# One transformer block on one core: all batches written out in place of loops of two, and the loads of the next stacks behind the store of the third group's row maxima

## The chip, the cores and the metric

The kernel runs on one core of a Trainium2 chip. The metric is the device time of one execution in microseconds (us). The kernel before takes 664.18 us, the median of three runs (663.45 to 664.81).

## What is computed

The reference is one block with adaptive layer norm for x of shape (8, 512, 128): attention with 16 heads of width 8, then a mixture of 8 experts of which each token uses two. Cut to what matters:

```python
mod = (silu(c) @ wmod).reshape(8, 6, 1, -1)            # sa, ca, ga, sb, cb, gb per batch
ga = sign(ga) * max(|ga|, 0.25);  gb likewise
h = layernorm(x) * (1 + ca) + sa
q, k, v = split(h @ w_qkv);  16 heads of width 8
attn = softmax(q @ k^T / sqrt(128));  o = attn @ v
x = x + ga * (o @ w_out)
h = layernorm(x) * (1 + cb) + sb
scores = softmax(h @ w_router);  top 2 of 8, made to sum to 1 -> comb
y = sum over experts e of comb[:, e] * ((silu(h @ w_gate[e]) * (h @ w_up[e])) @ w_down[e])
x = x + gb * y
```

Everything is float32. Attention is taken per batch of 512 tokens; the experts have 176 hidden units each, 8 x 176 = 1408 = 11 tiles of 128.

## The kernel before

**Two stages.** The first goes over the 8 batches and does attention, the projection, the second layer norm and the router. The second goes over the 8 batches again and does the experts. h2 and the router's weights pass between them through scratch memory in HBM (h2T_scr, combT_scr).

**A batch of the first stage** has 16 slots (SLOTS), four for each of four groups of four heads. A slot handles one chunk of 128 queries or keys of a group. In slot t TensorE makes four row scores (L1142: queries on the partitions, for the maxima) for the slot that lies eight further on (AHEAD), four column scores (L1155: keys on the partitions) for slot t, one of the tasks named in TASKS (transposes and projections for the next batch, output of the batch before), and the product of the probabilities with the values (L1169) for slot t - 1. VectorE takes the maximum of each row score (L853). ScalarE makes exp of each column score (L645) and empties the tasks' results. From slot 8 on the row scores are those of the next batch, so the next batch's stacks must be there by then.

**The stacks.** q and k of a batch are cut into three bf16 parts each, which lie under each other on the contraction axis: q_stack and k_stack, 128 partitions x 8 pairs of heads x 512. ScalarE and POOL make the parts in slots 1 to 4 of the batch before. SP stores them to q_scr and k_scr (L308, six stores each) and loads them back in stacked form (L317): first a quarter of each, 256 KB, counted on the semaphore stacked_first, then the rest, 768 KB each, counted on stacked. There are two stacks of each kind, for even and odd batches. TensorE waits for stacked_first ahead of the row scores of slot 0 of a batch (L1137) and for stacked ahead of those of slot 4 (L1139).

**The maxima.** They come in by rows but are needed by columns. POOL cuts a group's maxima into three parts (split_max), TensorE transposes them (L1098), ScalarE copies them out, stores them with its own DMA queue to max_scr (store_max, L657; groups 1, 2, 3 in slots 1, 5, 9, and group 0 of the next batch in slot 13) and a slot later reads them back into three free rows of q_stack (place_max, L664). The column scores of a group wait for that (L1152). The "third group" is group 2: stored in slot 5, read back in slot 6, used from slot 8.

**SP's order in a batch** (body, L391): wait for the last stacks to be loaded, store the parts of the next batch, load the next batch's stacks (load_stacks), in batch 0 load the expert gate weights, then wait for h2T of the batch before (keep_h2T, made in slot 10) and store it, and wait for combT of the batch before and store it.

**The second stage** has 11 tiles (k) per batch. For each TensorE makes gate and up (three float32r products each, product, L1254) and, three tiles behind (LAG), the down product into o_acc. ScalarE applies silu (L809), VectorE multiplies gate by up (L1022) and by the expert weights (L1032, operands in the space of the stacks), ScalarE makes the high part (hid_high, L789) and POOL the low part (hid_low, L601). When the 11 down products of a batch are done ScalarE scales y (L795, at k = 3 of the next block) and TensorE waits for that ahead of its next down product (L1267).

**The loops.** Each engine's program for both stages is written by over_batches (L277): batch 0, then a hardware loop (Fori) whose body holds the batches 2i+1 and 2i+2 and which runs three times, then batch 7. A body is called with its batch number, its parity, and whether it is the first or the last. In the loop the batch number is a register, so semaphore targets and addresses that hold it are computed by the engines' queues while they run; `isinstance(b, int)` tells in the code whether b is a number.

Of the kernel before, what the change touches and what calls it, by code (L numbers as in the profile page):

```python
# [13 lines left out]
def adaln_block(nc, x, w_qkv, w_out, w_router, w_gate, w_up, w_down, c, wmod, out):  # L14
    B, N, C = x.shape
# [103 lines left out]
    with ctx:  # L119
# [3 lines left out]
        def sem(name):  # L123
            return ctx.enter_context(nc.semaphore(name))
# [145 lines left out]
        s = {n: sem(n) for n in names}  # L270
# [5 lines left out]

        def over_batches(eng, body):  # L277

            body(0, 0, True, False)
            with eng.Fori(0, (B - 2) // 2) as i:  # L280
                body(2 * i + 1, 1, False, False)
                body(2 * i + 2, 0, False, False)
            body(B - 1, 1, False, True)

        def group(b, n):

            return NG * b + n
# [3 lines left out]
        def _(sp):  # L291
# [18 lines left out]
            def load_stacks(b, par):  # L310
                if isinstance(b, int) and b == 0:
                    sp.wait_ge(s["more_stored"], 16 * 4)
                sp.wait_ge(s["q_stored"], 16 * STORES * (b + 1))
                sp.wait_ge(s["k_stored"], 16 * STORES * (b + 1))
                for r0, r1, stacked in ((0, G // 2, "stacked_first"), (G // 2, PAIRS, "stacked")):
                    for stack_sb, scr in ((q_stack[par], q_scr), (k_stack[par], k_scr)):
                        sp.dma_start(stack_sb[:, r0:r1, :], scr.rearrange("a m r n -> (a m) r n")[:, r0:r1]).then_inc(s[stacked], 16)  # L317

            def stack(b, par):
                if not (isinstance(b, int) and b == 0):  # L320
                    sp.wait_ge(s["stacked"], 16 * LOADS * b)
                    sp.sem_inc(s["waited"])
                twice = [P, 2, N]
                store_parts(b, q_scr, (q_parts[:, Q_HIGH:Q_MID + 1], q_parts[:, Q_HIGH:Q_MID + 1], q_parts[:, Q_HIGH:Q_LOW + 1:Q_LOW - Q_HIGH]),
                            "q_mid", "q_split", "q_stored")
                store_parts(b, k_scr, (k_parts[:, K_HIGH:K_HIGH + 1].to_broadcast(twice), k_parts[:, K_MID:K_MID + 1].to_broadcast(twice),
                                       k_parts[:, K_LOW:K_HIGH + 1]), "k_mid", "k_split", "k_stored")
                load_stacks(b, par)

            def keep_h2T(b):  # L330
                sp.wait_ge(s["h2T_ready"], b + 1)
                sp.sem_inc(s["waited"])
                sp.dma_start(h2T_scr[bass.ds(b, 1)].rearrange("o c n -> c (o n)"), h2T[:]).then_inc(s["h2T_kept"], 16)

            def keep_combT(b):
                sp.wait_ge(s["combT_ready"], b + 2)
                sp.sem_inc(s["waited"])
                sp.dma_start(combT_scr[bass.ds(b, 1)].rearrange("o e n -> e (o n)"), combT[:]).then_inc(s["combT_kept"], 16)
# [7 lines left out]
            def fetch_h(b):  # L346

                if isinstance(b, int) and b == 0:
                    sp.wait_ge(s["attn_ready"], NO * (B - 1))
                else:  # L350
                    sp.wait_ge(s["h_split"], b)
                sp.wait_ge(s["h2T_kept"], 16 * (b + 1))
                sp.sem_inc(s["waited"])
                sp.dma_start(h_raw, h2T_scr[bass.ds(b, 1)].rearrange("o c n -> c (o n)")).then_inc(s["h_loaded"], 16)

            def spread_weights(b, k):

                if isinstance(b, int) and b == 0:
                    if k in (0, PAIRS):


                        sp.wait_ge(s["exp_done"], UNITS * (B - 1 if k == 0 else B))
                    if k == 0:
                        sp.wait_ge(s["combT_kept"], 16)
                else:
                    if k == 0:
                        sp.wait_ge(s["combT_kept"], 16 * (b + 1))
                    sp.wait_ge(s["weighed_ready"], KT * (b - 1) + k + 1)
                    sp.sem_inc(s["waited"])
                for e, r0, r1 in EXPERT_ROWS[k]:  # L370
                    sp.dma_start(spread[k][r0:r1], combT_scr[bass.ds(b, 1), e, :].to_broadcast([r1 - r0, N])).then_inc(s[f"spread{k}_loaded"], 16)
# [9 lines left out]
            def load_weights(i):  # L381

                if i:
                    sp.wait_ge(s["w_split"], i)
                if i < 2:
                    sp.dma_start(w_raw[:].rearrange("d (e h) -> d e h", e=E), (w_gate, w_up)[i].rearrange("e d h -> d e h")).then_inc(s["w_loaded"], 16)
                else:
                    sp.dma_start(w_raw[:].rearrange("p (k d) -> p k d", k=KT),
                                 w_down.rearrange("e h d -> (e h) d").rearrange("(k p) d -> p k d", p=P)).then_inc(s["w_loaded"], 16)

            def body(b, par, first, last):  # L391
                if not last:
                    stack(b + 1, 1 - par)
                if first:
                    load_weights(0)
                if last:
                    load_weights(1)
                    load_weights(2)
                if not first:
                    keep_h2T(b - 1)  # L400
                if last:
                    fetch_h(0)
                    for k in range(PAIRS):
                        spread_weights(0, k)
                if not first:
                    keep_combT(b - 1)

            over_batches(sp, body)


# [20 lines left out]
            for k in range(PAIRS, KT):  # L431
                spread_weights(0, k)
            over_batches(sp, block_body)
            store_result(B - 1)
            sp.wait_ge(s["result_stored"], 16 * B)
# [3 lines left out]
        def _(pool):  # L439
# [128 lines left out]
            def body(b, par, first, last):  # L568
# [22 lines left out]
                if not first:  # L591
                    score(b - 1)
                    denominator(b - 1)
                    combine(b - 1)

            over_batches(pool, body)


# [742 lines left out]
```

## Time and profile before

| | |
|---|---|
| median of 3 runs | 664.18 us (663.45 to 664.81) |
| profiled execution, its own time | 666.58 us |
| its span, first to last instruction | 664.8 us |
| granted TensorE clock, mean | 0.96 of full speed |
| busy: TensorE, VectorE, ScalarE, POOL | 609.4, 545.0, 443.4, 267.2 us |
| DMA moved | 65.58 MB, mean 99 GB/s |
| instruction packets, queues q8 and q14 | 14 and 30 |
| first stage, up to the last product with the values | about 450 us |

Busy time is the time in which an engine executed an instruction; waits, branches and register instructions don't count. PE is TensorE's matmul side, PEld its weight loads, DVE VectorE, ACT ScalarE, POOL GpSimd, SP the DMA-issuing engine; a name with q behind it (ACTq) is that engine's sequencer, which issues DMAs and does branches and register work. "Idle before" in a row is the engine's idle time just ahead of the instruction, and behind the arrow stands what ended it.

### The profile page before, as it was taken

The page shows a single profiled execution, that of the slowest core. Times are in us where ns is not written, and L with a number is a line of the kernel's source. Part 1 is how long each engine was busy: PE and PEld are TensorE (multiplying, and loading weights), DVE is VectorE, ACT ScalarE, POOL GpSimd, SP SyncE. Part 2 cuts the span into 40 slices and gives each one's busy share as a digit, 9 for nine tenths or more (in the row PEclk, how much of TensorE's full clock was granted, in tenths as well). Part 3 has the DMA queues.
Part 4 walks back from the last instruction along what each step waited for, and adds up shares of the span by engine and source line. Part 5 has one row for each costly group of instructions (what it writes and reads, how often), then busy time and mean ns, then how long its engine had stood idle before and what let it go on. Part 6 is the DMA issues. An engine that isn't in the chain of part 4 may idle for free.

```text
span 664.8 us, 12806 instructions
## 1 busy us (share of the span) xinstructions
PE 609.4 (92%) x3349; PEld 282.7 (43%) x3349; DVE 545.0 (82%) x1033; ACT 443.4 (67%) x843; POOL 267.2 (40%) x384
## 2 busy tenths in 40 slices
PE   4299999999999999999999999898899999999995
PEld 3112223322322322322322322226677777777773
DVE  3698889999998999998999999417788888888884
ACT  1207878878878778878778878875465555555552
POOL 4422012222222222222222212434576786786763
PEclk9757999999999999999999999979899999999997
DMA  7712604404304304304304301154244445344401
GB/s 187 178 56 61 210 4 97 131 19 97 131 20 97 129 18 97 130 19 97 129 18 97 130 19 47 50 156 142 80 129 157 129 136 149 126 142 142 133 26 32
DMA packets 49084, 65.58 MB, mean 99 GB/s; under 512 B 9544, under 2 KB 30544, under 8 KB 49040
## 3 DMA queue, kind: packets, MB, share of 16 engines
q1 hardware_dynamic: 46416, 64.32, 33.3%
q10 hardware_dynamic: 2624, 0.79, 0.5%
q8 instruction: 14, 0.23, 0.1%
q14 instruction: 30, 0.25, 0.1%
HBM read 47.26 MB, written 17.83 MB: 98 GB/s over the span
## 4 chain that ended last, share of the span: by engine, by line
PE 44%; issue 17%; POOL 16%; DVE 12%; ACT 6%; DMA 2%; SPq 1%; ACTq 1%; DVEq 1%; POOLq 0%
PE o_acc L1169 15%; POOL hid_lo L601 14%; PE s_row L1142 12%; PE s_col L1155 7%; DVE negmax L853 7%; ACT probs L645 4%; DVE probs L1032 2%; PE misc L1107 1%; POOL h_lo L607 1%; PE misc L1093 1%; PE misc L1090 1%; SPq L308 1%; PE misc L1123 1%; ACT oT L649 1%; PE misc L1119 1%
## 5 line engine op out<-in xcount | busy, mean ns | idle before, releaser
L853 DVE TENSOR_REDUCE negmax<-s_row 128x1 f32<-128x512 f32 x512 | 321.6, 682 | 37.9 <-PE s_row L1142 37.1
L645 ACT ACTIVATE probs<-s_col 128x512 f32<-128x512 f32 x512 | 273.6, 599 | 75.0 <-PE s_col L1155 72.0
L1142 PE MATMUL s_row<-k_stack,q_stack 64*128 64x512 bf16 x512 | 142.4, 403 | 23.8 <-DMA k_stack<-k_scr 11.0
L601 POOL TENSOR_TENSOR hid_lo<-probs,hid_hi 128x512 fp32r<-128x512 f32 x87 | 128.5, 1493 | 61.3 <-ACT hid_hi L789 61.3
L1169 PE MATMUL o_acc<-probs,v_aug 128*32 128x512 f32 x1024 | 138.1, 612 | 0.0
L1155 PE MATMUL s_col<-q_stack,k_stack 64*128 64x512 bf16 x512 | 132.3, 384 | 6.1 <-ACT probs L645 5.1
L789 ACT ACTIVATE hid_hi<-probs 128x512 fp32r<-128x512 f32 x88 | 55.6, 632 | 86.3 <-DVE probs L1032 86.0
L1142 PEld LDWEIGHTS s_row<-k_stack,q_stack 64*128 64x128 bf16 x512 | 36.0, 93 | 177.7 <-DVE negmax L853 138.5
L1032 DVE TENSOR_TENSOR probs<-probs,q_stack 128x512 f32<-128x512 f32 x56 | 62.3, 1112 | 15.6 <-POOL hid_lo L601 13.5
L509 POOL CAST negmax_parts<-negmax 128x16 bf16<-128x16 f32 x32 | 6.3, 196 | 166.9 <-DVE negmax L853 166.9
L1022 DVE TENSOR_TENSOR probs<-probs,s_col 128x512 f32<-128x512 f32 x88 | 59.6, 677 | 3.0 <-ACT probs L809 1.6
L809 ACT ACTIVATE probs<-s_row 128x512 f32<-128x512 f32 x88 | 51.5, 585 | 6.7 <-PE s_row L1258 5.9
L1155 PEld LDWEIGHTS s_col<-q_stack,k_stack 64*128 64x128 bf16 x512 | 38.1, 95 | 32.3 <-ACT probs L645 21.7
L1032 DVE TENSOR_TENSOR probs<-probs,k_stack 128x512 f32<-128x512 f32 x32 | 43.0, 1344 | 10.4 <-POOL hid_lo L601 9.8
L1256 PE MATMUL o_acc<-hid_hi,wd_hi 128*128 128x512 f32 x88 | 37.7, 428 | 5.6 <-POOL hid_lo L601 4.6
L1169 PEld LDWEIGHTS o_acc<-probs,v_aug 128*32 128x32 f32 x1024 | 20.2, 108 | 41.7 <-ACT probs L645 24.4
L1256 PE MATMUL s_row<-h_hi,wg_hi 128*128 128x512 f32 x88 | 36.2, 412 | 0.0
L1256 PE MATMUL s_col<-h_hi,wu_hi 128*128 128x512 f32 x88 | 35.3, 401 | 0.0
L1257 PE MATMUL o_acc<-hid_lo,wd_hi 128*128 128x512 f32 x88 | 35.3, 401 | 0.0
L1258 PE MATMUL o_acc<-hid_hi,wd_lo 128*128 128x512 f32 x88 | 35.2, 400 | 0.0
L1258 PE MATMUL s_col<-h_hi,wu_lo 128*128 128x512 f32 x88 | 35.1, 399 | 0.0
L1257 PE MATMUL s_col<-h_lo,wu_hi 128*128 128x512 f32 x88 | 35.0, 398 | 0.0
(134 smaller groups left out, 684.6 us busy)
## 6 DMA issues: line engine op xcount, KB each, us to landing
q_scr<-q_parts SPq DMA_DIRECT2D x48, 128.0 KB, 2.4
k_scr<-k_parts SPq DMA_DIRECT2D x48, 128.0 KB, 2.4
q_stack<-q_scr SPq DMA_DIRECT2D x8, 768.0 KB, 6.0
k_stack<-k_scr SPq DMA_DIRECT2D x8, 768.0 KB, 7.4
q_stack<-combT_scr SPq DMA_DIRECT2D x24, 256.0 KB, 3.3
k_stack<-combT_scr SPq DMA_DIRECT2D x16, 224.0 KB, 2.8
q_stack<-combT_scr SPq DMA_DIRECT2D x16, 192.0 KB, 2.8
q_stack<-combT_scr SPq DMA_DIRECT2D x16, 160.0 KB, 2.5
```

The source lines that it names most:

```text
L601: nc.gpsimd.tensor_tensor(hid_lo[k % HIDDEN][:], weighed[(par + k) % 2], hid_hi[k % HIDDEN][:], ALU.subtract).then_inc(s["hid_split"], 1)
L645: nc.scalar.activation(probs[t % 2][:, j, :], s_col[score_bank("col", u)][:], ACT.Exp, scale=INV_SCALE).then_inc(s["exp_done"], 1)
L789: nc.scalar.activation(hid_hi[k % HIDDEN][:], weighed[(par + k) % 2], ACT.Copy).then_inc(s["hid_high"], 1)
L853: nc.vector.tensor_reduce(negmax[n % 2][:, j, qc:qc + 1], s_row[score_bank("row", u)][:], AX.X, ALU.max, negate=True).then_inc(s["row_max" ...
L1022: nc.vector.tensor_tensor(gated[at], gate_act[at], u_ps[at], ALU.mult).then_inc(s["gated_ready"], 1)
L1032: nc.vector.tensor_tensor(weighed[at], gated[at], spread[k], ALU.mult).then_inc(s["weighed_ready"], 1)
L1142: nc.tensor.matmul(s_row[score_bank("row", u)][:], q_stack[par][at:at + KS, head // 2, P * qc:P * (qc + 1)], k_stack[par][at:at + KS, head ...
L1155: nc.tensor.matmul(s_col[score_bank("col", u)][:], k_stack[par][at:at + KS, head // 2, P * kc:P * (kc + 1)], q_stack[par][at:at + KS, head ...
L1169: last = nc.tensor.matmul(o_acc[VW * j:VW * (j + 1), :], values[:, kc, at:at + VW], probs[t % 2][:, j, :], start=first_of, stop=last_of)
L1256: nc.tensor.matmul(out_ps, w_hi[:, k, :], hi[:], start=start, stop=False)
L1257: nc.tensor.matmul(out_ps, w_hi[:, k, :], lo[:], start=False, stop=False)
L1258: return nc.tensor.matmul(out_ps, w_lo[:, k, :], hi[:], start=False, stop=stop)
```

## The change

All eight bodies of both stages are written out for every engine, and the batch number is a plain number in each. On SP the four loads of load_stacks for batch b wait, from batch 1 on, until group 2 of batch b - 1 has its maxima in max_scr.

```diff
         def over_batches(eng, body):
 
-            body(0, 0, True, False)
-            with eng.Fori(0, (B - 2) // 2) as i:
-                body(2 * i + 1, 1, False, False)
-                body(2 * i + 2, 0, False, False)
-            body(B - 1, 1, False, True)
+            for b in range(B):
+                body(b, b % 2, b == 0, b == B - 1)
...
                 sp.wait_ge(s["q_stored"], 16 * STORES * (b + 1))
                 sp.wait_ge(s["k_stored"], 16 * STORES * (b + 1))
+                if not (isinstance(b, int) and b == 0):
+                    sp.wait_ge(s["max_stored"], 16 * (group(b - 1, 2) + 1))
                 for r0, r1, stacked in ((0, G // 2, "stacked_first"), (G // 2, PAIRS, "stacked")):
```

## Rows read from the trace of the kernel before

**Rows 1.** The page, busy time, share of the span and instructions.

```profile
PE 609.4 (92%) x3349; PEld 282.7 (43%) x3349; DVE 545.0 (82%) x1033; ACT 443.4 (67%) x843; POOL 267.2 (40%) x384
```

**Rows 2.** Busy time by stretch, five batches: start:end, length, busy per engine, clock.

```profile
core 0: us, PE busy (x) PEld busy (x) DVE busy (x) ACT busy (x) POOL busy (x), PEclk, DMA share, GB/s
99.90:149.20 49.30, 47.67 (x314) 15.64 (x312) 45.34 (x97) 40.45 (x80) 13.24 (x34) 1.00 0.30 83
149.20:198.65 49.45, 47.63 (x314) 14.96 (x312) 45.32 (x97) 40.45 (x80) 13.17 (x34) 1.00 0.29 84
198.65:249.15 50.50, 47.91 (x314) 15.73 (x312) 45.41 (x96) 40.45 (x80) 13.21 (x34) 1.00 0.28 81
249.15:298.43 49.28, 47.58 (x314) 14.95 (x312) 45.31 (x96) 40.45 (x80) 13.18 (x34) 1.00 0.29 82
298.43:349.02 50.59, 47.94 (x314) 15.79 (x312) 45.42 (x97) 40.45 (x80) 13.23 (x34) 1.00 0.28 81
```

**Rows 3.** Timeline of ScalarE, start of batches 2 and 3: start, length, idle before.

```profile
149.40 1.08 ACT L645 ACTIVATE probs<-s_col 128x512 f32<-128x512 f32 x2 [0.22 <-PE s_col L1155]
...
200.08 1.08 ACT L645 ACTIVATE probs<-s_col 128x512 f32<-128x512 f32 x2 [1.46 <-PE s_col L1155]
```

**Rows 4.** The loop's line L280, 195 to 201 us: count, durations ns, starts.

```profile
L280 ACTq COMPARE_BRANCH  x1: 50/50/50, 197.3 to 197.3; - x1
L280 DVEq FUSED_REGOPS  x1: 85/85/85, 197.6 to 197.6; - x1
...
L280 ACTq FUSED_REGOPS  x1: 68/68/68, 199.9 to 199.9; - x1
```

**Rows 5.** DMA queues of 149.20:198.65, then of 249.15:298.43: packets, MB, share.

```profile
q8 instruction: 3, 0.05, 0.4%
...
q14 instruction: 2, 0.02, 0.1%
```

**Rows 6.** Busy time by stretch, two blocks of the expert stage.

```profile
488.40:513.05 24.65, 24.17 (x104) 18.66 (x104) 21.03 (x24) 13.64 (x25) 18.11 (x13) 1.00 0.44 138
513.05:537.65 24.60, 24.12 (x104) 18.64 (x103) 20.84 (x24) 13.62 (x25) 17.97 (x13) 1.00 0.44 142
```

**Rows 7.** Timeline of TensorE, first down product of blocks 6 and 7.

```profile
611.81 0.40 PE L1258 MATMUL s_col<-h_hi,wu_lo 128*128 128x512 f32 x1
612.38 0.47 PE L1256 MATMUL o_acc<-hid_hi,wd_hi 128*128 128x512 f32 x1 [0.17 <-ACT probs L795]
...
636.44 0.39 PE L1258 MATMUL s_col<-h_hi,wu_lo 128*128 128x512 f32 x1
636.84 0.47 PE L1256 MATMUL o_acc<-hid_hi,wd_hi 128*128 128x512 f32 x1
```

**Rows 8.** Timeline of VectorE, tile 1 of blocks 6 and 7.

```profile
610.30 0.69 DVE L1032 TENSOR_TENSOR probs<-probs,q_stack 128x512 f32<-128x512 f32 x1 [0.20 <-DVE probs L1022]
...
634.76 0.69 DVE L1032 TENSOR_TENSOR probs<-probs,q_stack 128x512 f32<-128x512 f32 x1
```

**Rows 9.** Timeline, batch 3: the third group's store, the first load of SP.

```profile
216.08 0.33 ACTq L657 DMA_DIRECT2D max_scr<-negmax_T  x1
...
216.37 0.34 SPq L317 DMA_DIRECT2D q_stack<-q_scr  x1
```

**Rows 10.** DMAs issued in 215:219, last row in 165:168: KB, us to landing.

```profile
k_stack<-k_scr SPq DMA_DIRECT2D x1, 768.0 KB, 7.3
...
k_stack<-k_scr SPq DMA_DIRECT2D x1, 256.0 KB, 4.2
...
max_scr<-negmax_T ACTq DMA_DIRECT2D x1, 12.0 KB, 1.4
...
k_stack<-k_scr SPq DMA_DIRECT2D x1, 256.0 KB, 5.5
```

**Rows 11.** Timeline of TensorE: first row scores of batch 4.

```profile
224.86 0.44 PE L1142 MATMUL s_row<-k_stack,q_stack 64*128 64x512 bf16 x2
```

**Rows 12.** Busy time by stretch, end of the first stage.

```profile
433.90:440.70 6.80, 6.54 (x24) 0.75 (x23) 1.49 (x15) 3.74 (x9) 3.64 (x6) 0.50 0.89 259
```

## The prediction

> **What bounds the kernel now.** I read the busy table first. TensorE is busy for 92% of the span [rows 1], so the question for every edit is whether it gives TensorE its next matmul sooner. Then I cut the attention stage into batches, each from one batch's first transpose (L1086, slot 0) to the next batch's, and asked for the busy time of each stretch. TensorE is busy for about 47.6 of 49.3 us in each, at a full granted clock, VectorE for 45.3 and ScalarE for 40.5 [rows 2]. So a batch is close to TensorE's own work, but all three engines are so nearly full that a hole of a microsecond on any of them is not made up.
>
> The same rows show something that belongs to the loop. The stretches last 49.30, 49.45, 50.50, 49.28 and 50.59 us [rows 2]. The third begins within a slot of the place where the loop over pairs (1,2), (3,4), (5,6) jumps back for the first time, the fifth where it jumps back for the second time. There are only two taken jumps, since the third test falls through. Their TensorE work is the same (x314).
>
> ScalarE's timeline shows the hole. Where one body simply follows another, the first exp of a batch starts after an idle time of 0.22 us; at the jump it is 1.46 us [rows 3]. The loop's own instructions explain it: ScalarE's branch starts at 197.3 and takes 50 ns, and its next instruction comes at 199.9, about 2.5 us later, while VectorE's branch of the same moment is followed by its next instruction at 197.6 [rows 4]. ScalarE had two exps queued ahead of the branch, which cover about half of that gap; the rest is the 1.2 us.
>
> **The change part by part.**
>
> *The loops written out, attention stage.* Two taken jumps go. Worked out: (50.50 + 50.59) - 2 x 49.30 = 2.49 us [rows 2]. Measured against 49.45 it is 2.19, against 49.28 it is 2.53; I take 2.49. What is late next once the hole is gone is what is late in the other stretches, TensorE itself, and that is already in the 49.30. The Trainium skill ("Runtime: NRT & Kernel Launch", section "Instruction fetch mechanics") says that a taken branch to code outside the two resident pages must wait until the target page has been fetched, and that crossing a page boundary in straight code is mostly hidden; by that rule the trace's 2.5 us on ScalarE are a page fetch, and writing the code out removes it.
>
> *What straight code costs instead.* Bodies 3 to 6 of the attention loop now have to be fetched for the first time, TensorE's too. In the stretch 149.20 to 198.65, the loop's first pass, TensorE's code arrives in three packets of the queue q8; in 249.15 to 298.43, the same body in its second pass, only two packets of the other engines' queue q14 come [rows 5]. The two stretches last 49.45 and 49.28 us, and the first-pass stretch before them 49.30 [rows 2]. So a body that is fetched costs 0.02 to 0.17 us more than one that is resident, and four bodies cost 0.1 to 0.7 us. I take 0.3. The packets are 0.05 MB in a batch, beside some 4 MB of data.
>
> *The loops written out, expert stage.* Cut at the start of the first y scaling (L795) of each block, a block without a jump lasts 24.65 us and one with a taken jump 24.60 [rows 6]. The jumps cost nothing there: ScalarE is busy for only 13.6 us of a block and TensorE for 24.1. But another cost of the loop shows. The last block is already written out. In block 6, inside the loop, TensorE passes from the last up product to the first down product in 612.38 - 611.81 = 0.57 us and waits 0.17 for the y scaling; in the last block it takes 636.84 - 636.44 = 0.40 and no wait is listed [rows 7]. The cause lies on VectorE: in the loop the multiplication by the expert weights (L1032, k = 1) starts after 0.20 us of idle time behind the gating (L1022), in the last block none is listed [rows 8]. In the loop body the wait of L1029 for a register's value is an instruction of its own ahead of it. With constants it can sit in the multiplication. Six blocks (1 to 6) get the form of the last one: 6 x 0.17 = 1.0 us. Bounds: nothing, if another wait of the block takes it over (TensorE's second stall in a block is for POOL's hid_lo), and 6 x 0.26 = 1.6 us, an estimate from half again of the 0.17 for that second stall. I take 1.0.
>
> *Register arithmetic elsewhere.* In attention the loop bodies compute each wait's value in the engines' queues. It runs while their instructions are busy. No row shows a stall from it; I take nothing, with 0 to -0.5 us as bounds.
>
> *The new wait of SP.* It stands in front of the four stack loads, behind the two waits for the stores of q and k. Behind it on SP are the four loads, in the first batch also the weight load (704 KB, needed six batches later), and then the wait for h2T, which comes some 15 us after the loads; nobody else waits in SP's queue. In batch 3 ScalarE issues the third group's store at 216.08 and SP the first load at 216.37 [rows 9]. The store lands 1.4 us after its issue [rows 10], so about 217.5, and counting 0.3 us from landing to the next issue, the loads start at 217.8: 1.4 us later than now. In the first batch (store at 69.0, loads at 70.1 now) the shift is about 0.5 us. Is there room? The half that is needed first lands last with k_stack's 256 KB: issued 0.38 us behind the first load, landing 4.2 us later in this batch and 5.5 in the worst one [rows 10]. That gives 217.8 + 0.4 + 4.2 = 222.4, at worst 223.7. TensorE's first row scores of the next batch start at 224.86 [rows 11]. Room: 2.5 us, at worst 1.2. The second half (768 KB, 7.3 us [rows 10]) would be there at about 226.5 and is read four slots after 224.86, over 12 us later. The cost is zero. It is covered by TensorE's slots 6 and 7, and if that cover went, each microsecond of lateness would cost one in each of seven batches.
>
> What could the wait bring? It takes the loads' packets out of the way of the small store and of the read back into q_stack that follows it. The column scores of slot 8 need that read. No instruction of the trace is listed as waiting for it, and the slots have the same length in the batch where the store took 2.5 us instead of 1.4. So the gain is zero too.
>
> **Sum.** -2.49 + 0.3 - 1.0 + 0 = -3.2 us. Against the profiled execution (666.58 us, of which 664.8 are the span and 1.8 lie around it) that is 663.4; that execution was 2.4 us above the median of the runs, 664.18, to which I apply the same difference: 661.0 us.
>
> **The rivals.**
>
> *The hole is not the jump's.* Only ScalarE shows it; VectorE's restart after 0.4 us [rows 4] speaks for a cheap branch. Then the attention gain is nil and -1.0 + 0.3 leaves 663.5, no measurable change. Against it: both long stretches, and only they, hold a taken jump. The Trainium skill ("Advanced Engine Details and Errata", "Control Flow Timing") puts a compare-and-branch at about 108 ns, by which the four jumps of a program would be worth an estimated 0.4 us; ScalarE's 50 ns agree with the instruction itself, but the 2.5 us behind it do not agree with the idea that this is all.
>
> *Code that comes late.* Straight code must be fetched for every body. If ScalarE, whose queue is short, missed each of its blocks of code as it missed the jump's target, 1.2 us a time, one miss in each of the four newly fetched bodies would cost 4.8 us and turn the sum into +1.6 less the 0.3 already counted: 665.5. It decides from three misses on (3 x 1.2 = 3.6 against the 3.2 gained). Against it: the first-pass stretches fetched their code and lasted 49.30 and 49.45 [rows 2, 5].
>
> *The loads come too late (the other side).* Place: TensorE's row scores at slot 8. It decides once the first k half lands over 2.5 us later than reckoned, for instance if it took as long as the second half's 7.3 us, because the read of q_stack and all four loads now start together. It would land at 225.5, 0.6 us late; with the row scores then behind in each of seven batches, and VectorE with no slack to make it up, 7 x 0.6 = 4.5 us, which gives 665.5. With 2 us late it is 675. Against it: four loads start together now too, at 4.2 to 5.5 us.
>
> *The clock.* Between the stages TensorE's granted clock is 0.50 for 6.8 us with TensorE busy for 6.54 [rows 12]; it fell after a stretch in which TensorE had waited for ScalarE and POOL several times. At full clock that work would take about half, so such a dip is worth up to 3 us. A program that is shorter by 3 us may meet it a little differently, longer or shorter: 658.5 or 663.5.
>
> **How the numbers follow.** What can be told from no change here is 0.2%, 1.3 us. My forecast, 661.0 with its own range 659.6 to 662.6, gets 0.68. The clock 0.14 (0.10 of it still faster, 0.03 the same, 0.01 slower). The hole that isn't the jump's 0.11 (0.09 same, 0.02 slower). Late code 0.04 and late loads 0.03, both slower. So faster 0.78, same 0.12, slower 0.10. The range takes in the bounds of the terms (-2.5 + 0.1 - 1.6 - 0.5 = -4.5 gives 659.7, and -2.2 + 0.7 - 0 = -1.5 gives 662.7) and reaches toward the clock's cases: 658.9 to 663.7.
>
> **What would show it.** Right: ScalarE's first exp of every batch after 0.2 us of idle time; all six stretches between 49.2 and 49.5 us; more packets in the instruction queues, twice as many in q8; blocks 1 to 6 of the expert stage at 24.46 us; first loads about 1.4 us behind the third group's store in each batch, and no instruction waiting for k_stack besides the one at the start. Wrong: a stretch of over 50 us anywhere, or row scores that wait for a DMA in slot 8 (then the loads decide), or blocks that still last 24.6 us (then another wait has taken the 0.17).

## The result: 656.0 us, 8.7 us less than before

Over 20 runs of each, the changed kernel takes 656.02 us (653.28 to 663.60) and the kernel before 664.75 us (661.19 to 668.04). The ratio is 0.9877 with a 95% interval of 0.9857 to 0.9897, that is 6.8 to 9.5 us less. The forecast was 3.2 us less, 661.0 us, with a range down to 658.9. The sign was right, and so were the two gains that the sum named, the jumps and the experts. A third, which the sum put at nothing, was the largest.

The profiled execution took 655.2 us with a span of 653.6. These are its rows, in the views of before. First the busy table, which answers to [rows 1]: TensorE is busy for 8.4 us less with the same number of instructions.

```profile
PE 601.0 (92%) x3349; PEld 277.1 (42%) x3349; DVE 544.0 (83%) x1033; ACT 443.7 (68%) x843; POOL 267.0 (41%) x384
```

The attention batches, cut at the same transposes as in [rows 2] (start:end, length, busy time and count by engine, clock, DMA share, GB/s); the third and the fifth used to hold a taken jump. The last row is the low-clock stretch between the stages, which was 6.8 us long in [rows 12]:

```profile
99.63:148.24 48.61, 47.11 (x314) 14.64 (x313) 45.27 (x97) 40.48 (x80) 13.18 (x34) 1.00 0.30 84
148.24:196.85 48.61, 47.11 (x315) 14.63 (x313) 45.27 (x97) 40.47 (x80) 13.18 (x34) 1.00 0.30 85
196.85:245.45 48.60, 47.10 (x314) 14.63 (x312) 45.25 (x97) 40.47 (x80) 13.18 (x34) 1.00 0.30 84
...
294.06:342.66 48.60, 47.10 (x314) 14.64 (x313) 45.27 (x97) 40.47 (x80) 13.16 (x34) 1.00 0.29 84
421.90:425.30 3.40, 3.21 (x14) 1.02 (x14) 0.00 (x0) 3.12 (x6) 0.04 (x1) 0.51 0.13 46
```

ScalarE's first exp at the place of the former jump (start, length, idle time before it; [rows 3] had 1.46 us), then the instruction queues of the whole program, from the page:

```profile
196.95 1.08 ACT L644 ACTIVATE probs<-s_col 128x512 f32<-128x512 f32 x2 [0.21 <-PE s_col L1154]
```

```profile
q8 instruction: 27, 0.44, 0.3%
q14 instruction: 28, 0.22, 0.1%
```

A block of the expert stage, and TensorE's first down product in the block that was numbered 6 in [rows 7]; and SP's first load behind the third group's store, with its landing, which answer to [rows 9] and [rows 10]:

```profile
576.58:601.04 24.46, 24.13 (x105) 18.65 (x104) 20.78 (x24) 13.63 (x26) 17.99 (x13) 1.00 0.47 142
```

```profile
601.45 0.40 PE L1257 MATMUL s_col<-h_hi,wu_lo 128*128 128x512 f32 x1
601.86 0.47 PE L1255 MATMUL o_acc<-hid_hi,wd_hi 128*128 128x512 f32 x1
```

```profile
212.71 0.33 ACTq L656 DMA_DIRECT2D max_scr<-negmax_T  x1
214.15 0.33 SPq L316 DMA_DIRECT2D q_stack<-q_scr  x1
```

```profile
k_stack<-k_scr SPq DMA_DIRECT2D x1, 256.0 KB, 4.6
```

What the reader is to see: all five stretches are equal, and they are not 49.3 us long, as forecast, but 48.6. TensorE's own busy time in a stretch fell from 47.6 to 47.1 us with the same number of matmuls, so part of what it waited before must have been booked as busy time of its matmuls. The 11.2 us by which the two profiled spans differ are, cut at the first product with the values in each batch: start 0.3, last slots of batch 0 0.2, two jumps 2.5, batches 1 to 6 another 6 x 0.67 = 4.0, batch 7 with the shorter low-clock stretch 2.5, six blocks 1.0, the end at a better clock 0.7. So 4.0 us are not in the forecast's sum. The last batch and the end, some 3 us together, are for the most part the clock (an estimate from the low-clock stretch, 3.4 us instead of 6.8, and from the end). The medians, which average the clock over 20 runs, leave 8.7.

The chain of waits of one batch shows where to look for the missing 4.0 us, but not their size. These are its shares by line, before and then after. "issue" is time in which an engine waited for nothing the profile names: 14.4% of 49.45 us is 7.1 us, of which 1.26 are the hole at the jump; 4.4% of 48.61 is 2.1. The issue time fell by 3.7 us beyond the hole, while the batch got only 0.84 us shorter: most of the rest moved to the shares of TensorE and VectorE.

```profile
by line: PE o_acc L1169 24.2%; PE s_row L1142 15.8%; issue 14.4%; PE s_col L1155 11.7%; DVE negmax L853 9.8%; ACT probs L645 7.6%; PE misc L1107 2.4%; PE misc L1093 2.2%; PE misc L1090 2.1%; PE misc L1123 2.0%; ACT oT L649 1.6%; DVE r_witho
```

```profile
by line: PE o_acc L1168 26.6%; PE s_row L1141 18.9%; DVE negmax L852 13.8%; PE s_col L1154 12.1%; ACT probs L644 5.9%; issue 4.4%; PE misc L1106 2.4%; PE misc L1092 2.2%; PE misc L1089 2.2%; PE misc L1122 2.0%; DVE x_all L879 1.4%; PE misc 
```

### The profile page after: what moved, and what is told of

Its sections match the earlier page's. It is cut to its first block, busy times and chain, and to the rows that moved or that the text cites. A ratio compares the mean times of both kernels' runs of the same rounds, so it can differ in the third digit from the quotient of the medians.

```text
span 653.6 us, 10459 instructions
## 1 busy us (share of the span) xinstructions
PE 601.0 (92%) x3349; PEld 277.1 (42%) x3349; DVE 544.0 (83%) x1033; ACT 443.7 (68%) x843; POOL 267.0 (41%) x384
## 4 chain that ended last, share of the span: by engine, by line
PE 47%; DVE 20%; POOL 15%; ACT 8%; issue 6%; DMA 1%; SPq 1%; POOLq 0%; DVEq 0%; ACTq 0%
PE o_acc L1168 16%; PE s_row L1141 14%; POOL hid_lo L600 11%; DVE negmax L852 8%; DVE probs L1031 7%; PE s_col L1154 7%; ACT probs L644 3%; ACT hid_hi L788 3%; POOL h_lo L606 2%; PE misc L1106 1%; SPq L305 1%; PE misc L1122 1%; PE misc L1092 1%; PE misc L1089 1%; DVE probs L1021 1%
## 5 line engine op out<-in xcount | busy, mean ns | idle before, releaser
L644 ACT ACTIVATE probs<-s_col 128x512 f32<-128x512 f32 x512 | 273.4, 598 | 66.0 <-PE s_col L1154 62.9
L1154 PE MATMUL s_col<-q_stack,k_stack 64*128 64x512 bf16 x512 | 127.8, 381 | 3.3 <-ACT probs L644 2.7
L1154 PEld LDWEIGHTS s_col<-q_stack,k_stack 64*128 64x128 bf16 x512 | 36.2, 95 | 23.0 <-ACT probs L644 15.2
```

The lines of the kernel that those rows point to most:

```text
L644: nc.scalar.activation(probs[t % 2][:, j, :], s_col[score_bank("col", u)][:], ACT.Exp, scale=INV_SCALE).then_inc(s["exp_done"], 1)
L1154: nc.tensor.matmul(s_col[score_bank("col", u)][:], k_stack[par][at:at + KS, head // 2, P * kc:P * (kc + 1)], q_stack[par][at:at + KS, head ...
```

## The experiments

In each, the five attention stretches from the second batch on are added up as the most exact measure: 249.12 us before, 243.03 after. The stretches are from the one profiled execution of each kernel. Times are medians, ratios are to the kernel before on the same chip.

**unroll_only.** All loops written out, without the new wait. Against the kernel after:

```diff
-                if not (isinstance(b, int) and b == 0):
-                    sp.wait_ge(s["max_stored"], 16 * (group(b - 1, 2) + 1))
```

> All bodies written out, without the new wait of SP. Theory R (the loop's registers cost time in every body): all of the gain stays; attention batches last 48.6 us as in the changed kernel, blocks 24.47, time about 656 us, same as the changed kernel within 0.3%. Theory W (the later loads give the unexplained 0.67 us of a batch): batches last 49.2 to 49.3 us, time about 660 us.

Measured: 656.94 us, ratio 0.9872 (0.9838 to 0.9907). Five stretches: 243.00.

```profile
148.93:197.53 48.60, 47.09 (x314) 14.64 (x313) 45.24 (x97) 40.49 (x80) 13.21 (x34) 1.00 0.30 85
```

Within the interval the whole gain is there without the wait.

**wait_only.** The loops of before, with the new wait.

```diff
                 sp.wait_ge(s["k_stored"], 16 * STORES * (b + 1))
+                if not (isinstance(b, int) and b == 0):
+                    sp.wait_ge(s["max_stored"], 16 * (group(b - 1, 2) + 1))
```

> The loops of two stay, only the new wait of SP is added. Theory R: no change, batches of 49.3 us and two of 50.5, time within 0.2% of the kernel before. Theory W: batches of 48.6 us and two of 49.9, time about 660.7 us (664.7 - 4.0).

Measured: 664.01 us, ratio 0.9997 (0.9970 to 1.0024), five stretches 248.71, two of them (50.37, 50.35) with a jump. The wait alone moves nothing. The 4.0 us belong to the writing out.

**hinted_jump.** The loops of before, and the branch's target is fetched ahead.

```diff
-            with eng.Fori(0, (B - 2) // 2) as i:
+            with nc.Fori(0, (B - 2) // 2, engines=bass.OrderedEngineSet([eng.engine]), hint_back_edge=True) as i:
```

> The loops of two stay, with an instruction at the head of each pass that has the code at the jump's target fetched ahead. Theory J (the hole at the jump is ScalarE's missing code): the two stretches of 50.5 us fall to 49.3, ScalarE's idle time there from 1.46 to about 0.22 us, time 2.5 us below before (-0.37%). If the hole is something else in the loop's turn: no change.

Measured: 665.85 us, ratio 1.0015 (0.9986 to 1.0044); stretches 50.49, 49.26, 49.27, 49.26, 49.26. First the loop's own line on ScalarE (against [rows 4]), then ScalarE's first exp behind the jump and a stall in the first stretch.

```profile
L280 ACTq COMPARE_BRANCH  x1: 68/68/68, 198.9 to 198.9; - x1
...
L280 ACTq FUSED_REGOPS  x1: 68/68/68, 199.2 to 199.2; - x1
```

```profile
200.42 1.08 ACT L645 ACTIVATE probs<-s_col 128x512 f32<-128x512 f32 x2 [0.22 <-PE s_col L1155]
```

```profile
126.61 0.09 PEld L1155 LDWEIGHTS s_col<-q_stack,k_stack 64*128 64x128 bf16 x1 [1.09 <-DMA q_stack<-max_scr]
126.61 0.39 PE L1155 MATMUL s_col<-q_stack,k_stack 64*128 64x512 bf16 x1 [0.80 <-DMA q_stack<-max_scr]
```

ScalarE resumes 0.3 us after the branch instead of 2.5, and the stretches with a jump are as long as the others: the hole was the fetch of the jump's target. The gain of 2.5 us does not show in the time, and the profiled execution has two places where it went. One is a stall of 1.2 us in batch 1 (the PE row above), where the store of the third group's maxima took 3.06 us and its read-back 6.56 us to land. The larger one is in the last batch, behind the loop: ScalarE idles for 2.26 us and nothing in the profile says for what; then TensorE runs for 3.0 us at a granted clock of 0.52. That slot lasts 6.64 us instead of 3.17.

```profile
415.50 0.60 ACT L645 ACTIVATE probs<-s_col 128x512 f32<-128x512 f32 x1 [2.26 <-issue]
```

```profile
417.40:420.40 3.00, 3.00 (x13) 1.89 (x12) 0.86 (x2) 1.15 (x3) 0.00 (x0) 0.52 0.00 0
```

Of the thirteen kernels profiled only the two that fetch the branch's target ahead have such a hole there. Two packets of the instruction queue q14 come at 414.0 and 416.2 us, so code that arrives late is likely; that the fetch ahead causes it is not shown. Whether the timed runs lose at the same places can't be seen.

**swapped_waits.** The loops of before. In the exps, the row maxima and the experts' multiplication by the weights, the wait named first is named last.

```diff
-                act.wait_ge(s["col_ready"], UNITS * b + u + 1)
                 if j == 0 and not (isinstance(b, int) and b == 0 and t < 2):
                     act.wait_ge(s["pv_done"], SLOTS * b + t - 1)
+                act.wait_ge(s["col_ready"], UNITS * b + u + 1)
```

> The loops of two stay; where exp (L645), the row maximum (L853) and the weighing (L1032) have several waits, the one that comes true last is now named last, so that it should sit on the instruction itself and the early ones on instructions of the sequencer. Theory R, in the form that only the late wait on an instruction of its own costs time: batches 0.3 to 0.6 us shorter (48.7 to 49.0), blocks 24.47 in place of 24.63, time 3 to 5 us below before, with the two holes of 1.2 us still there. If the register arithmetic itself costs the time, or the addresses: no change in either.

Measured: 665.63 us, ratio 1.0024 (0.9999 to 1.0049). Five stretches 247.77, blocks 24.84.

```profile
247.85:297.01 49.16, 47.43 (x314) 14.86 (x313) 45.23 (x97) 40.64 (x80) 13.16 (x34) 1.00 0.29 83
533.54:558.40 24.86, 24.32 (x105) 18.61 (x104) 20.84 (x24) 13.58 (x26) 18.32 (x13) 1.00 0.49 137
```

The expected 3 to 5 us did not come. Attention gets shorter by 0.1 to 0.5 us a batch, with the registers still there, and the blocks longer by 0.2, which takes back what attention gives. So where a wait stands matters, both ways. It led to the theory for the rest: an instruction holds one wait. Its others stand ahead of it in the queue as instructions of their own. The wait that is met last costs time if it is one of these. In attention's loop, where values come from registers, the wait named first is the one that stands alone, and the kernel names the late one first (col_ready, row_ready). In straight code it is the one named last.

The experts' loop does not follow the first rule. There the swap put the late wait (gated_ready) ahead of the multiplication by the weights instead of on it, and in most tiles that multiplication starts 0.13 us behind the gating (here 536.67 - 536.53 = 0.14), where before it was 0.03 to 0.04. This is why the blocks got longer:

```profile
535.86 0.67 DVE L1022 TENSOR_TENSOR probs<-probs,s_col 128x512 f32<-128x512 f32 x1
536.67 0.69 DVE L1032 TENSOR_TENSOR probs<-probs,q_stack 128x512 f32<-128x512 f32 x1
```

For attention the trace shows it by line for the exps of one batch, before (L644 is the line of pv_done) and then after (L643):

```profile
L644 ACTq ALU_OP  x13: 35/35/35, 156.2 to 196.1; - x13
L644 ACTq EVENT_SEMAPHORE  x2: 17/17/17, 152.7 to 178.5; - x2
```

```profile
L643 ACTq EVENT_SEMAPHORE  x16: 17/17/17, 151.6 to 196.4; - x16
```

After, pv_done stands alone 16 times, long met, and col_ready sits on the exp. Before, pv_done stands alone twice; in the other 14 the instruction that computes pv_done's value (13 ALU_OP, one FUSED_REGOPS) stands ahead of the exp and holds the wait for col_ready. The Trainium skill ("Perfetto Trace Analysis", "Identifying Dependency Chains") says that an instruction that waits for several engines may get EventSemaphore instructions ahead of it; the rows agree (16 of them in a batch after).

**late_wait_alone.** unroll_only with these waits of the exps and row maxima named in the other order, so that in straight code too the late one stands alone. Of the two edits, the one on VectorE:

```diff
-                dve.wait_ge(s["row_ready"], UNITS * b + u + 1)
                 if qc == 0 and j == 0 and not (isinstance(b, int) and b == 0 and n < 2):
                     dve.wait_ge(s["max_split"], 4 * (group(b, n) - 1))
+                dve.wait_ge(s["row_ready"], UNITS * b + u + 1)
```

> Straight code without the new wait, as unroll_only (656.94 us, batches 48.60 us). One thing is changed: in the exps (L645 of before) and the row maxima the two waits are named in the other order, so that the one that is met last (col_ready, row_ready) goes to the sequencer as an instruction of its own, which the profile's list of waits shows for the loop kernels. Theory A (a late wait that stands alone, ahead of its instruction, costs the start of that instruction; the 4.0 us of the result come from where the waits sit): slots 0, 9, 11 and 12 go back from 2.70, 2.96, 3.07, 2.87 towards 2.81, 3.11, 3.15, 2.96 us, batches 48.9 to 49.1, the kernel 2 to 3 us slower than unroll_only: 659 to 660. Theory B (it is the register arithmetic of the loop itself that costs, wherever the waits sit): batches stay at 48.6, the kernel at 657.

Measured: 659.28 us, ratio 0.9925 (0.9899 to 0.9951). Five stretches 243.97, each 48.80. VectorE's first row maximum of a group in this kernel, then in unroll_only:

```profile
147.55 1.89 DVE L850 TENSOR_REDUCE negmax<-s_row 128x1 f32<-128x512 f32 x3 [0.29 <-PE s_row L1139]
```

```profile
148.81 1.89 DVE L850 TENSOR_REDUCE negmax<-s_row 128x1 f32<-128x512 f32 x3 [0.22 <-PE s_row L1139]
```

The same instruction starts 0.07 us later. Slots 0, 11 and 12 are 2.78, 3.13 and 2.94 us long instead of 2.70, 3.08 and 2.87, which makes a batch 0.2 us longer, with no register involved; slot 9 stayed at 2.96. Theory A holds, though the 0.2 is less than the 0.3 to 0.5 expected. Against unroll_only's ratio the kernel is slower by 3.5 us, with intervals that overlap a little; the traces show 1.4 of it (7 x 0.2).

**swapped_all.** The loops, with the late wait named last in all two-wait instructions of attention (exp, row maximum, ScalarE's evacuations, the weighing on TensorE), and the experts as before.

> The loops of before, with registers and jumps. In every instruction of attention that has two waits (exp, row maximum, ScalarE's evacuations of q, k, the maxima and combT, TensorE's weighing) the one that is met last is named last, so that it sits on the instruction; the experts' weighing is left as before. Theory A: a loop can have most of the gain without being written out: batches 48.8 to 48.95 us besides the two jumps (50.0 to 50.2), blocks 24.63, the kernel 2 to 2.8 us faster than before: 661.5 to 662.2. Theory B (register arithmetic): batches 49.3, no change, 664.2.

Measured: 664.10 us, ratio 0.9999 (0.9970 to 1.0027). Five stretches 248.27.

```profile
99.31:148.19 48.88, 47.46 (x315) 15.56 (x313) 45.27 (x97) 40.61 (x80) 13.25 (x34) 1.00 0.30 84
148.19:197.57 49.38, 47.41 (x314) 14.82 (x312) 45.26 (x97) 40.61 (x80) 13.18 (x34) 1.00 0.29 84
```

An undisturbed batch is 48.88 us long, as expected, so the order of naming gives 0.4 of the 0.67, slots 0, 9, 11 and 12 being 2.70, 2.98, 3.08 and 2.87 us long, as in after. But the time did not move, where 2 to 2.8 us were expected. Both jumps are still there. In batch 3 the read-back took 7.22 us to land, and TensorE's column scores waited 0.5 us for it. In batches 2, 4 and 6 slot 9 lasted 3.27 us instead of 2.98, since ScalarE's exp behind the store of the maxima started 0.28 us late; the profile names no cause, and it stays open.

**registers_no_jump.** Bodies 1 to 4 in one-pass loops (registers, no taken jump), 5 and 6 with plain numbers.

```diff
-            with eng.Fori(0, (B - 2) // 2) as i:
-                body(2 * i + 1, 1, False, False)
-                body(2 * i + 2, 0, False, False)
+            for pair in range(2):
+                with eng.Fori(pair, pair + 2, 2) as i:
+                    body(2 * i + 1, 1, False, False)
+                    body(2 * i + 2, 0, False, False)
+            body(5, 1, False, False)
+            body(6, 0, False, False)
```

> Bodies 1 to 4 of both loops stand in two loops of one pass each (registers, no taken jump), bodies 5 and 6 are written out with plain numbers; the new wait is left out. Theory A and B alike (the gain per batch comes with the constants, the rest is the jump): batches 1 to 4 last 49.3 us with no stretch over 50, batches 5 and 6 48.6; expert blocks 1 to 4 24.63, blocks 5 and 6 24.46. Sum: 2.5 (two jumps) + 2 x 0.67 + 2 x 0.17 = 4.2 us faster than before, 660.0. Rival (the gain per batch comes from straight code as such, fetched once and never jumped in): batches 1 to 4 at 48.6 too, 657.

Measured: 660.81 us, ratio 0.9954 (0.9927 to 0.9982), that is 1.2 to 4.8 us less; the expected 4.2 lie inside. Two attention stretches and two blocks, each time first with registers and then with numbers:

```profile
198.47:247.81 49.34, 47.70 (x315) 15.67 (x313) 45.38 (x97) 40.45 (x80) 13.25 (x34) 1.00 0.29 84
...
297.09:345.98 48.89, 47.10 (x314) 14.63 (x313) 45.35 (x97) 40.52 (x80) 13.19 (x34) 1.00 0.30 84
530.83:555.46 24.63, 24.13 (x104) 18.64 (x103) 20.87 (x24) 13.63 (x26) 18.08 (x13) 1.00 0.48 142
579.95:604.43 24.48, 24.15 (x105) 18.61 (x104) 20.78 (x24) 13.63 (x25) 18.02 (x13) 1.00 0.43 142
```

In one program, bodies with registers last 49.3 and 24.63 us and bodies with numbers 48.9 and 24.48 (of the 48.9, 0.3 lie in slot 1 at the change of form; the next slots are those of unroll_only), although all are fetched once and none is jumped to. The rival (straight code as such) is out.

**address_registers.** unroll_only, but in batches 1 to 4, which stand in loops of one pass for this, the addresses come from a register; all waits are constants. One of the places:

```diff
-                    row = x_all[:, bass.ds(b, 1), :, :].rearrange("p o k c -> p (o k c)")
+                    row = x_all[:, bass.ds(at_batch(b), 1), :, :].rearrange("p o k c -> p (o k c)")
```

> As unroll_only, but in batches 1 to 4 the addresses that depend on the batch (hT, h2T, x, the scalings) come from a register, while every wait has a constant. Theory A: slots 7 and 1, which the swap of two waits in the loop did not shorten, are long because of instructions whose address comes from a register and which therefore carry no wait: in batches 1 to 4 slot 7 3.14 and slot 1 4.05 us, together +0.2 to +0.25 a batch, batches 48.8 against 48.6 in 5 and 6, and blocks unchanged but for yT (24.46 to 24.55); the kernel 0.8 to 1.2 us slower than unroll_only, 658. Rival (addresses cost nothing, only waits do): 48.6 in all.

Measured: 656.81 us, ratio 0.9888 (0.9849 to 0.9927). Batches 1 to 4 last 48.73 us, 0.13 more than in unroll_only. Batch 5, with plain addresses, lasted 50.27 instead of 48.6: its read-back of the third group's maxima took 7.0 us to land, and the slot that waited for it 4.88 us instead of 3.21. First batches 4 and 5, then the sum x1 on VectorE, in this kernel and in the one after:

```profile
245.37:294.10 48.73, 47.24 (x315) 14.67 (x313) 45.26 (x97) 40.55 (x80) 13.19 (x34) 1.00 0.29 84
294.10:344.37 50.27, 47.45 (x314) 14.78 (x313) 45.36 (x97) 40.37 (x80) 13.16 (x34) 1.00 0.29 82
```

```profile
166.75 1.29 DVE L867 TENSOR_REDUCE negmax<-s_row 128x1 f32<-128x512 f32 x2 [0.22 <-PE s_row L1156]
168.18 0.69 DVE L894 TENSOR_TENSOR x_all<-misc,x_all 128x512 f32 x1
```

```profile
167.07 1.29 DVE L852 TENSOR_REDUCE negmax<-s_row 128x1 f32<-128x512 f32 x2 [0.22 <-PE s_row L1141]
168.38 0.69 DVE L879 TENSOR_TENSOR x_all<-misc,x_all 128x512 f32<-128x512 f32 x1
```

The gap between them is 168.18 - 168.04 = 0.14 us against 168.38 - 168.36 = 0.02. With an address in a register the wait sits on the instruction that computes the address; in the kernel before the gap is 0.13 as well. It is the only place in the batch where this address costs anything. Slot 7 came out as expected (3.15 us), slot 1 did not: it stayed at 3.92.

**late_attached.** The kernel after, with the late wait put on the instruction in five more places, the experts' two multiplications on VectorE among them. The second of these:

```diff
+                    if not (first and k < 2):
+                        dve.wait_ge(s["hid_split"], i - 1)
                     dve.wait_ge(s["gated_ready"], i + 1)
                     dve.wait_ge(s[f"spread{k}_loaded"], 16 * len(EXPERT_ROWS[k]) * (b + 1))
-                    if not (first and k < 2):
-                        dve.wait_ge(s["hid_split"], i - 1)
```

> The kernel after, with waits named in another order in five places, so that the one met last sits on its instruction and the others stand alone: the gating multiplication (L1021 of after: up_ready instead of gate_acted on it, 88 times), the multiplication by the weights (L1031: hid_split instead of gated_ready, 86 times), the column scores (L1154: exp_done instead of max_loaded, 31 times), the row scores (L1141: row_max instead of the loads, 15 times), the gate product of k = 0 (L1255). Theory A (order of waits): TensorE's stalls for hid_lo in a block (1.3 us in four blocks) shrink, the 14.6 us that VectorE idles for hid_lo in four blocks shrink by 40 times 0.06 to 0.1 us; blocks 24.46 to 24.2-24.4, batches 48.61 to 48.4-48.55. The kernel 0.5 to 2.5 us faster than after: 654.5 in the middle. Theory B (the order matters only where an instruction starts late for nothing else; here it is all covered): no change, 656.

Measured: 658.52 us, ratio 0.9896 (0.9869 to 0.9922); batches 48.60 as in after, blocks 24.69 against 24.46. One more block, not counted here, lasted 25.89 us: VectorE idled for 0.44 us in it with nothing named. VectorE in a block, this kernel and then after:

```profile
529.72 1.76 DVE L1031 TENSOR_TENSOR probs<-probs,q_stack 128x512 f32<-128x512 f32 x1 [0.61 <-POOL hid_lo L600]
531.40 0.68 DVE L1021 TENSOR_TENSOR probs<-probs,s_col 128x512 f32<-128x512 f32 x1
532.16 0.70 DVE L1031 TENSOR_TENSOR probs<-probs,q_stack 128x512 f32<-128x512 f32 x1
```

```profile
528.37 1.67 DVE L1031 TENSOR_TENSOR probs<-probs,q_stack 128x512 f32<-128x512 f32 x1 [0.70 <-POOL hid_lo L600]
529.97 0.67 DVE L1021 TENSOR_TENSOR probs<-probs,s_col 128x512 f32<-128x512 f32 x1
530.67 0.69 DVE L1031 TENSOR_TENSOR probs<-probs,q_stack 128x512 f32<-128x512 f32 x1
```

The expected gain did not come (654.5 was its middle), for two reasons that the rows show. The first multiplication does start 0.09 us earlier behind POOL's hid_lo, but POOL's next subtraction is running by then, beside which it takes 1.76 us instead of 1.67, and so it ends no earlier. In the next one the wait met last is gated_ready, and that now stands alone: 532.16 - 532.08 = 0.08 us behind the gating multiplication instead of 530.67 - 530.64 = 0.03. Which wait is late changes from one k to the next, and the order of after is the better one.

**loop_all.** The loops, with swapped_all's order, hinted_jump's fetch and the new wait together.

> The loops of before with the three things together that the single experiments gave: swapped_all's order of waits, hinted_jump's fetch ahead of the back edge, and the new wait of SP, which keeps the read-back of the third group's maxima out of the stack loads. Theory A: batches 48.88 us in all, no stretch over 49.0, no read-back that TensorE waits for; blocks 24.63. Sum 2.5 + 6 x 0.39 = 4.8 us faster than before, 659.3. Rival (a loop gives back what the waits save, as swapped_all did): single batches of 49.4 or more, 662 to 664.

Measured: 661.28 us, ratio 0.9928 (0.9902 to 0.9954), 4.4 us less than before on that chip. Five stretches 244.26, all alike:

```profile
101.19:150.04 48.85, 47.38 (x314) 15.52 (x312) 45.28 (x97) 40.62 (x80) 13.25 (x34) 1.00 0.30 84
...
296.61:345.45 48.84, 47.38 (x314) 15.52 (x313) 45.27 (x97) 40.61 (x80) 13.25 (x34) 1.00 0.29 83
```

The expected time was 659.3. The 4.4 us are close to the 4.8 that the traces of the single runs add up to, and they are half of the change's gain with the loops kept. The last batch has the hole of hinted_jump again, 1.87 us on ScalarE, in a slot that is 1.4 us longer than in after, and two packets of q14 beside it (413.6 and 415.9 us):

```profile
415.20 1.09 ACT L647 ACTIVATE probs<-s_col 128x512 f32<-128x512 f32 x2 [1.87 <-PE s_col L1157]
```

**after_again.**

> The kernel after itself, unchanged, beside the others of this call: 656.0 us as in its first runs, batches 48.61. Its distance to unroll_only (656.94 us, no new wait) was 0.9 us with intervals of 1.3 and 2.3 us, so that the worth of the new wait is open; if it comes out at 656.9 or more, the wait is worth nothing on this evidence.

Measured: 657.26 us, ratio 0.9890 (0.9848 to 0.9931), five stretches 243.01. No version tried is faster than the kernel after by more than the intervals allow.

## Why the prediction was wrong

**Failed: "Register arithmetic elsewhere", taken as nothing with 0 to -0.5 us as bounds.** It measured 6 x 0.67 = -4.0 us, and 0.2 more in batch 0. The reason given ("it runs while their instructions are busy") looked at the arithmetic. What costs most is that the wait which is met last does not sit on its instruction. Of the 0.67 us, the order of waits accounts for 49.27 - 48.88 = 0.39 (swapped_all) and the register address of x1 for 0.13 (address_registers). Of the other 0.15, 0.10 are in slot 1: 4.02 in swapped_all, where the loop's registers are, and 3.92 in address_registers, where only addresses are registers. So it hangs on a wait or on arithmetic that neither changed; which one stays open.

That the term is not nothing could have been found. For the experts the prediction compared a block of the loop with the written-out one [rows 7, 8] and priced the difference; for attention it did not make the same comparison. Body 0 was written out too. Slot 9 in bodies 0 and 1 of the kernel before, cut at the weighing's first matmul:

```profile
78.94:81.90 2.96, 2.82 (x19) 0.74 (x17) 2.54 (x5) 2.88 (x7) 0.00 (x0) 1.00 0.43 131
127.10:130.20 3.10, 2.89 (x19) 0.74 (x17) 2.68 (x5) 2.90 (x7) 2.60 (x6) 1.00 0.02 4
```

The same matmuls take 0.15 us longer in the loop, and after the change the slot is 2.96 in all bodies. Six such slots are 0.9 us, already beyond the bound of 0.5. The full 4.0 could not have been read off in this way, since most other slots of body 0 do less work than those of the loop (it has no batch before it). "No row shows a stall from it" was wrong as well: such a delay carries no releaser's name and is filed under issue, or inside a wait that is listed as 0.29 instead of 0.22.

**Right: the two jumps, -2.49.** hinted_jump and registers_no_jump take the two long stretches back to 49.3 us, without and with another fetch of the code. The rival "the hole is not the jump's" is out.

**Too high: the refetch, +0.3.** Twice the packets in q8 (27 against 14), and the five stretches are equal to 0.01 us. It measured nothing.

**Right: the experts, -1.0.** Blocks 24.46 us; TensorE passes to the first down product in 601.86 - 601.45 = 0.41 us with no wait listed.

**Nearly right: the new wait, 0.** The loads start 1.44 to 1.84 us behind the store (forecast 1.4 among the signs; the working had 1.7, with 0.3 us from the landing to the issue, which measured 0.08). The first k half lands 1.4 to 2.9 us before its reader (forecast 1.2 to 2.5), but only 0.7 in two batches of after_again. wait_only shows no gain. But the slack on the other side was called safe too early. Without the wait the read-back of the third group's maxima landed over 4.5 us after its issue in 41 of the 56 batches profiled (eight kernels), and in 3 of them TensorE waited for it, for 0.5 to 1.6 us. With the wait it landed after 2.3 to 4.2 us in all 35 batches of the five kernels that have it. Once, in late_attached, the first k half was 0.4 us late instead. From these traces the wait is worth an estimated 0.3 to 0.4 us a program (1.2, 0.5 and 1.6 us over eight programs, less 0.5 once in five), too little for these runs: 656.02 and 657.26 with it, 656.94 without.

**The clock** was a rival and added to the profiled pair, 3.4 us of low clock between the stages instead of 6.8. It does not make the gain: at a mean granted clock of 0.973, eight executions of the kernel before (beside the experiments) have a median of 662.0 us and four of the kernel after 654.7, 7.3 us less. The terms measured add up to 7.7 (2.5 + 4.2 + 1.0); the other 1.0 us of the medians is inside the interval. In the kernel after, late code and late loads did not happen.

## What to carry to other kernels

Before a loop is written out, compare a body in the loop with a written-out copy of it (the first or the last pass) slot by slot, on every stage. Where both do the same work, the difference times the passes is a first estimate of the gain, whatever its cause. Where an instruction on a full engine has several waits, see which one sits on it. The one that is met last should, and in these programs the order in which they are named decides: with constants the one named last stood alone, in attention's loop the one named first, in the experts' loop not. So look at the trace for which one it is. Where another wait is late in another pass, leave it alone.

## What was not expected of the hardware

- With the late wait on the instruction VectorE started 0.02 to 0.04 us behind the end of its previous instruction; with the same wait ahead of it, 0.08 to 0.14 us. Behind TensorE's row score the idle time grew from 0.22 to 0.29 us.
- A taken branch with its target fetched ahead resumed on ScalarE after 0.3 us, without that after 2.5. In both kernels with the fetch ahead ScalarE had a hole of 1.9 to 2.3 us in the last batch, behind the loop.
- VectorE's product of two SBUF tensors took 0.69 us alone and 1.67 to 1.78 us while POOL's subtraction ran, and an earlier start brought no earlier end. The Trainium skill ("SBUF — State Buffer", "Who interferes with whom") says that a VectorE instruction with two SBUF inputs contends with a GpSimd instruction that reads SBUF; these rows agree.
- The third group's store of 12 KB landed after 1.35 to 1.9 us in 85 of the 91 batches profiled and after 2.5 to 3.1 us in six. The small read-back behind it landed after 2.3 to 4.2 us in the 49 batches where it was issued at most 0.65 us behind the first large load, and after 4.6 to 7.2 us in 41 of the 42 where it was issued 0.7 us or more behind it.
